# Attention with a causal convolution: whole groups of values, the second query stack in another bank, and the finished output read earlier

## The reference

```python
xn = _rms_norm(x, g_norm) * (1.0 + scale) + shift     # scale, shift = split(cond @ W_emb + b_emb)
q, k, v = heads(xn @ W_qkv)
q = _rms_norm(q, g_q);  k = _rms_norm(k, g_k)
o = softmax(q @ k.T * d ** (-0.5)) @ v                # per head
x = x + (o + o @ W_out)
x = x + causal_depthwise_conv(x, cond) + b            # 4 taps along the rows
```

## Time and profile before

| | before |
|---|---|
| median of 3 runs | 2447.68 us |
| the profiled execution, its own time | 2451.33 us |
| its span, first to last instruction | 2449.4 us |
| PE, share of the span busy | 95% |
| DVE | 84% |
| ACT | 73% |
| POOL | 29% |
| mean granted TensorE clock | 0.989 |

### The profile page before, as it was taken

How to read it: one execution, slowest core, us unless ns; L and a number is a source line. 1 busy time by engine, 2 the same in 40 slices (tenths; PEclk the granted TensorE clock), 3 DMA queues, 4 the chain that set the end, 5 groups by cost and what they waited for, 6 DMA issues and landing times.

```text
span 2449.4 us, 53026 instructions
## 1 busy us (share of the span) xinstructions
PE 2318.2 (95%) x20410; PEld 1499.9 (61%) x20410; DVE 2062.1 (84%) x3212; ACT 1789.7 (73%) x2693; POOL 702.9 (29%) x483
## 2 busy tenths in 40 slices
PE   5799898988899999999999999999999999999889
PEld 0455555555466666666666666666666666666678
DVE  7768988888878888888888888888888888888877
ACT  5467788888777778777777787777777777777732
POOL 1022333332333323333333333333222232322210
PEclk9899999999999999999999999999999999999999
DMA  8999999899999999999999999999998988888971
GB/s 348 312 226 229 193 176 200 182 189 227 204 199 181 204 192 212 181 197 234 200 218 185 213 186 202 195 187 227 192 191 173 182 168 161 176 164 173 193 193 56
DMA packets 1234731, 484.91 MB, mean 198 GB/s; under 512 B 1139632, under 2 KB 1197872, under 8 KB 1232048
## 3 DMA queue, kind: packets, MB, share of 16 engines
q1 hardware_dynamic: 1234480, 481.53, 94.2%
HBM read 137.20 MB, written 56.66 MB: 79 GB/s over the span
## 4 chain that ended last, share of the span: by engine, by line
PE 57%; DVE 19%; issue 8%; ACT 7%; SPq 3%; DMA 2%; POOL 1%; ACTq 0%; POOLq 0%; DVEq 0%
PE proj L1000 33%; PE scores L944 9%; PE values L963 8%; DVE p_pair L1544 7%; DVE neg L1535 7%; PE proj L1033 4%; ACT p_pair L1193 3%; ACT late L1185 2%; DMA w_sb<-w_dram 2%; SPq L746 2%; DVE stage L1566 1%; DVE bias L1538 1%; PE values L976 1%; DVE stage L1570 1%; PE misc L1051 1%
## 5 line engine op out<-in xcount | busy, mean ns | idle before, releaser
L1000 PE MATMUL proj<-w_sb,xn_sb 128*128 128x384 f16 x6144 | 1036.2, 328 | 26.9 <-DMA w_sb<-w_dram 19.6
L1000 PEld LDWEIGHTS proj<-w_sb,xn_sb 128*128 128x128 f16 x6144 | 593.3, 98 | 433.0 <-issue 50.5
L1185 ACT ACTIVATE late<-scores,bias,l_scale 128x1024 f32<-128x1024 f32 x512 | 615.1, 1202 | 311.9 <-DVE bias L1538 292.3
L1544 DVE TENSOR_TENSOR p_pair<-late,p_pair 128x1024 f16<-128x1024 f32 x512 | 616.6, 1246 | 161.3 <-ACT p_pair L1193 160.9
L1535 DVE TENSOR_REDUCE neg<-scores 128x1 f32<-128x1024 f32 x512 | 623.6, 1218 | 113.0 <-PE scores L944 109.8
L1193 ACT ACTIVATE p_pair<-late 128x1024 f16<-128x1024 f32 x512 | 509.8, 1045 | 0.0
L963 PE MATMUL values<-pT,v_pair 128*64 128x256 f16 x6144 | 387.3, 276 | 13.1 <-ACT inv_all L1253 13.1
L944 PE MATMUL scores<-late 64*128 64x512 f16 x3072 | 376.6, 378 | 15.9 <-ACT late L1185 15.5
L963 PEld LDWEIGHTS values<-pT,v_pair 128*64 128x64 f16 x6144 | 317.7, 110 | 93.9 <-issue 74.9
L1435 POOL TENSOR_TENSOR rs<-ms,power 128x16 f32<-128x16 f32 x63 | 183.2, 2908 | 351.8 <-DVE ms L1558 351.5
L1033 PE MATMUL proj<-late,wo 128*128 128x256 f16 x2304 | 267.5, 273 | 3.7 <-issue 3.7
(11 more groups left out here) (179 smaller groups left out, 1925.9 us busy)
## 6 DMA issues: line engine op xcount, KB each, us to landing
w_sb<-w_dram SPq DMA_DIRECT2D x121, 384.0 KB, 4.1
o_dram<-oT_pair SPq DMA_DIRECT2D x124, 128.0 KB, 2.4
out<-late SPq DMA_DIRECT2D x54, 256.0 KB, 2.7
x_in<-in_x SPq DMA_DIRECT2D x25, 512.0 KB, 4.3
late<-in_x SPq DMA_DIRECT2D x25, 512.0 KB, 4.4
wq_raw<-in_L_cond_W_qkv SPq DMA_DIRECT2D x8, 1536.0 KB, 11.5
late<-o_dram SPq DMA_DIRECT2D x12, 1024.0 KB, 6.2
xn_dram<-late SPq DMA_DIRECT2D x21, 512.0 KB, 3.2
```

The lines of the kernel that those rows point to most:

```text
L1000: last = nc.tensor.matmul(proj[:, t % 2, 0:6 * DH], xn_sb[:, t, i * K + c, :], w_sb[:, c, j, :], start=(c == 0 and i == j == 0), stop=(c = ...
L1185: nc.scalar.activation(prob[:, h, :], scores[:, h, :], ACT.Exp, bias=bias[:, s:s + 1], scale=const["l_scale"][:, 0:1], accum_out=total[:, ...
L1544: nc.vector.tensor_tensor(p_pair[:, s % 4, 1, :], prob[:, h, :], p_pair[:, s % 4, 0, :], ALU.subtract).then_inc(lo_done, 1)
```

## The change

It touches the orders of PE, ACT and SP; those of DVE and POOL stay as they are.

- `attend` takes a range of chunks instead of a part. With `outs` a group is done whole (48 matmuls in a row): group 3 of the unit before at pair 2, group 0 at pair 4, group 1 at pair 6, group 2 at the end of pair 7. The halves at the ends of pairs 1, 3 and 5 and the one behind the scores of pair 0 are gone. Units 0 to 7 keep the halves, and the last unit's group 3 too.
- The second stack of half 1 goes into `misc`, behind the whole group 2 at pair 7's end. The projection's wait for it is gone with `fins`, and the stack before it in `misc` no longer waits for `read_out` of half 1.
- `out_transposes` of half 1 moves from pair 6 to pair 4's end, `read_out` of it to the end of ACT's pair 4, `store_out` of it from pair 7 to pair 6 (in front of the loads there).
- `read_inverses` of group 1 moves on ACT from the front of pair 5 to behind its exponents and high parts.

```diff
@@ -864,7 +864,7 @@
                             keep_xn(v)
                         elif xs:
                             store_xn(v)
-                    if p == 6 and fins and last:
+                    if p == 6 and fins:
                         store_out(T - 1, 1 - par, 1)
                     if last and p == 1:
                         load_last_oT(0)
@@ -880,8 +880,6 @@
                         if more and not gives_early(u):
                             load_w(w + 1, 2)
                     if p == 7:
-                        if fins and not last:
-                            store_out(T - 1, 1 - par, 1)
                         if more and not gives_early(u):
                             load_w(w + 1, 3)
                         if not last:
@@ -948,15 +946,15 @@
                             if i == 1 and n == 1:
                                 last.then_inc(qk_done, 1)
 
-            def attend(u, g, par, part):
+            def attend(u, g, par, c0=0, c1=K):
                 n = NG * u + g
-                if part == 0:
+                if c0 == 0:
                     pe.wait_ge(all_ev, n + 1)
                     if g == 0:
                         pe.wait_ge(v_lo, 2 * u + 2)
                     for i in range(4):
                         pe.wait_ge(pT_in[4 * (g % 2) + i], 16 * (2 * u + g // 2 + 1))
-                for c in range(part * KH, (part + 1) * KH):
+                for c in range(c0, c1):
                     for i, j in ((0, 0), (1, 0), (0, 1)):
                         for h in range(2):
                             first = 4 * (g % 2) + h
@@ -965,7 +963,7 @@
                                 v_pair[:, par, 2 * c + h, DH * i:DH * i + DH],
                                 pT[:, first:first + 3:2, j * K + c, :],
                                 start=(c == 0 and i == j == 0), stop=(c == K - 1 and j == 1))
-                if part == 1:
+                if c1 == K:
                     last.then_inc(pv_done, 1)
 
             def inverses(u, g):
@@ -984,7 +982,8 @@
                     if early and t == 1:
                         pe.wait_ge(h_ev, 3 * w - 1)
                     elif t == (2 if early else 0):
-                        need(pe, h_ev, 3 * w)
+                        if fins is None:
+                            need(pe, h_ev, 3 * w)
                     if fins is not None and t < 2:
                         pe.wait_ge(y_ev, 2 * fins + t + 1)
                     if static(w) and w % K == 0:
@@ -1078,6 +1077,7 @@
                 w, T = u + 1, u - K
                 begun = not (static(u) and u == 0)
                 last = u + 1 == U
+                was_whole = u > K
                 for p in range(K):
                     if gives_early(u) and p == 7:
                         project(w + 1, 0, 0, 4)
@@ -1086,9 +1086,11 @@
                         keep_clock(12)
                     score(u, p, par)
                     if p % 2 == 0 and p >= 4:
-                        attend(u, (p - 4) // 2, par, 1)
-                    elif p % 2 == 0 and begun:
-                        attend(u - 1, 2 + p // 2, 1 - par, 1)
+                        attend(u, (p - 4) // 2, par, 0 if outs else KH, K)
+                    elif p == 0 and begun and not was_whole:
+                        attend(u - 1, 2, 1 - par, KH, K)
+                    elif p == 2 and begun:
+                        attend(u - 1, 3, 1 - par, 0 if outs else KH, K)
                     if p % 2 == 1 and p >= 3:
                         inverses(u, (p - 3) // 2)
                     elif p == 1 and begun:
@@ -1098,9 +1100,9 @@
                             project(w + 1, 1, 0, 4)
                         elif not outs:
                             keep_clock(8)
-                        stacks(w, 1, 1, misc[:], (f_ev, 2 * T) if fins else (h_ev, 3 * w + 1))
-                        stacks(w, 1, 0, proj[:, 0, :], (y_ev, 2 * T + 1) if outs else
-                               (qkv_ev, K * w + (9 if gives_early(u) else 7)))
+                        stacks(w, 1, 1, misc[:], (h_ev, 3 * w + 1))
+                        if not outs:
+                            stacks(w, 1, 0, proj[:, 0, :], (qkv_ev, K * w + (9 if gives_early(u) else 7)))
                     if qkv:
                         for t, q0, q1 in (later_quarters if has_early(u) else quarters)[p]:
                             project(w, t, q0, q1, T - 1 if fins else None)
@@ -1115,8 +1117,6 @@
                             out_product(T, par, 0, 1, oT_in, xr, ())
                         else:
                             out_product(T, par, 1, p - 6, oT_in, xr, free1)
-                            if fins and p == 6:
-                                out_transposes(T - 1, 1, (h_ev, 3 * w + 1) if qkv else (f_ev, 2 * T - 1))
                     if last and p < 4:
                         hh = p // 2
                         out_product(T, par, hh, p % 2, oT_in, last_xr[0],
@@ -1127,18 +1127,22 @@
                         if p >= 6:
                             add_x(p - 6, last_xr[1])
                     if qkv and outs and p == 5:
-                        stacks(w, 0, 0, misc[:], (f_ev, 2 * T - 1 if fins else 0))
+                        stacks(w, 0, 0, misc[:], (f_ev, 2 * T if fins else 0))
                         stacks(w, 0, 1, proj[:, 1, :], (qkv_ev, K * w + 8))
                     if fins and p == 1 and not last:
-                        out_transposes(T - 1, 0, (k_ev, u + 1))
-                    if fins and p == 4 and last:
+                        out_transposes(T - 1, 0, (h_ev, 3 * u + 3))
+                    if fins and p == 4:
                         out_transposes(T - 1, 1, (f_ev, 2 * T - 1))
-                    if p % 2 == 1 and p >= 3:
-                        attend(u, (p - 3) // 2, par, 0)
-                    elif p == 1 and begun:
-                        attend(u - 1, 3, 1 - par, 0)
+                    if p % 2 == 1 and p >= 3 and not outs:
+                        attend(u, (p - 3) // 2, par, 0, KH)
+                    elif p == 1 and begun and not outs:
+                        attend(u - 1, 3, 1 - par, 0, KH)
+                    elif p == 7:
+                        attend(u, 2, par)
+                        if qkv:
+                            stacks(w, 1, 0, misc[:], (k_ev, w + 1))
                     if last and p == 1:
-                        out_transposes(T - 1, 0, (k_ev, u + 1))
+                        out_transposes(T - 1, 0, (h_ev, 3 * u + 3))
                     if qkv and not outs and p == 5:
                         stacks(w, 0, 0, misc[:], (qkv_ev, 0))
                         stacks(w, 0, 1, proj[:, 1, :], (qkv_ev, K * w + 8))
@@ -1153,7 +1157,6 @@
             stacks(0, 1, 1, misc[:], (h_ev, 1))
             stacks(0, 1, 0, proj[:, 0, :], (qkv_ev, K - 1))
             in_units(unit, pe)
-            attend(U - 1, 2, 1, 1)
             for hh in range(2):
                 tail_product(0, hh, K - 1)
             tail_product(1, 0)
@@ -1161,9 +1164,9 @@
             tail_transposes(U - K - 1, 0)
             tail_product(1, 1)
             tail_transposes(U - K - 1, 1)
-            attend(U - 1, 3, 1, 0)
+            attend(U - 1, 3, 1, 0, KH)
             tail_transposes(U - K, 0)
-            attend(U - 1, 3, 1, 1)
+            attend(U - 1, 3, 1, KH, K)
             for i in range(2, K):
                 T = U - K + i
                 tail_product(i, 0)
@@ -1298,7 +1301,7 @@
                         read_y(T, 0)
                     if last and p == 4:
                         read_y(T, 1)
-                    if p % 2 == 1 and p >= 3:
+                    if p in (3, 7) or p == 5 and not outs:
                         read_inverses(u, (p - 3) // 2)
                     elif p == 1 and begun:
                         read_inverses(u - 1, 3)
@@ -1315,8 +1318,6 @@
                         if qkv:
                             read_projection(w, 7)
                             squares(w, 1, (h_ss, 2 * w + 1))
-                        if fins and last:
-                            read_out(T - 1, 1)
                     if p == 6:
                         if outs and not last:
                             read_y(T, 0)
@@ -1335,16 +1336,16 @@
                     high(u, p, 1)
                     if 4 <= u < K and p in (1, 3):
                         wo_high(2 * u - 8 + p // 2)
+                    if p == 5 and outs:
+                        read_inverses(u, 1)
                     if qkv and not outs and p == 6:
                         high_halves(w, 1)
                     if p % 2 == 0 and p >= 4:
                         o_high(u, (p - 4) // 2)
                     elif p % 2 == 0 and begun:
                         o_high(u - 1, 2 + p // 2)
-                    if p == 6 and fins and not last:
-                        read_out(T - 1, 1)
                     if qkv and p == 7:
-                        read_stacks(w, 1 - par, 1, 0, 3, proj[:, 0, :])
```

(3 more changed lines are left out.)

## The result

| | before | after |
|---|---|---|
| median of 5 runs | 2448.12 us (2445.06 to 2454.39) | 2428.83 us (2425.20 to 2437.39) |
| the profiled execution, its own time | 2451.33 us | 2425.20 us |
| its span | 2449.4 us | 2423.4 us |
| PE, share busy | 95% | 95% |
| DVE, ACT, POOL | 84%, 73%, 29% | 85%, 74%, 29% |

The ratio is 0.9922, with a 95% interval from 0.9908 to 0.9935: 19 us less (16 to 22.5 by the interval), where 19 was forecast, and clear of the 0.5% too. The two profiled executions lie further apart (26 us) than the medians; of that, 4.9 us are gone before unit 8 starts, where both kernels are the same, so a sum must not be read off the spans alone.

What follows compares the result with a forecast made beforehand. PE was taken as the bound, busy 69.93 of 70.39 us a unit. 22 x 1.01 - 15 x 0.15 + 0.1 - 1.5 = 18.6, rounded 19 us, so the median 2447.68 becomes 2428.7; range 2423 to 2442.

Steps and rivals of the forecast that it cites:

- The price of halves and wholes: On PE, 24 matmuls take 1.43 us and 48 take 2.74; each of three joins saves 0.12 a unit.
- The pairs: PE, pairs 0 to 7: 8.33, 8.06, 11.07, 7.62, 10.54, 8.34, 7.09, 8.33 us; sum 69.38 against 70.39.
- The wait, 0.62: In pair 7, PE's stacks no longer wait for ACT's read of the output: 0.62 us less in a unit.
- What is late next: Whether DVE and ACT, in pairs made shorter or longer, come late for PE; a new wait of 0.15 us at pair 1.
- the lag of 1.0 at pair 6: DVE's first maximum of pair 6 starts 2.54 us behind its scores instead of 1.51.
- its 23.92 us on DVE: DVE's chain from pair 6's first maximum to pair 1's goes on taking 23.92 us.
- the 0.15 at pair 1: PE's output transposes in pair 1 wait for DVE, 0.1 to 0.3 us, taken as 0.15, in units 9 to 23 only.
- The spare at pair 7's scores: Pair 6's second exponent ends at 6.63, pair 7 starts at 7.09: no wait, 0.3 us to spare after a semaphore's latency.
- The rival in which DVE is 0.4 later (8 us): DVE's lag costs 2 us at pair 7's scores and 6 at pair 1's transposes: 2437; chance of the lag 0.18.
- The weights: Pair 0's last quarter lands at 11.6, wanted at 12.7 us after pair 7's scores; no steady wait, 1.5 lost in all.
- the four units: Units 15, 16, 23 and 27, whose last quarter of weights lands late or just in time: 0.4 us more each.
- Edges: Unit 8 takes 0.5 us longer (between 0 and 1.04); the last unit keeps 0.6 of the half taken from pair 0.

Runs made afterwards that it cites:

- group 0 in halves: Changed kernel with group 0 done in halves again (24 matmuls at pair 3's end, 24 behind pair 4's scores): 2426.1 us, one run.
- the earlier output alone: Kernel before, with only the output's second half turned, read and stored earlier: 2447.3 us, ratio 0.9999 (0.9986 to 1.0012).
- inverses in front: Changed kernel with ACT reading group 1's inverses in front of pair 5's exponents again: 2434.1 us, one run.
- whole groups alone: Kernel before, with only the groups done whole as in the change: 2437.6 us, ratio 0.9958 (0.9943 to 0.9973).
- store at pair 7: Changed kernel with the store of the output's second half back in front of the last quarter of weights in pair 7: 2430.2 us, one run.
- quarter behind both stores: Changed kernel with the stores of the output and of group 1 both in front of the last quarter of weights in pair 7: 2433.6 us, one run.

## Why the prediction was right, point by point

*The price of halves and wholes:* 1.43, 2.74, 0.12 a join: right, by the timeline and by group 0 in halves. The comparison of 57 with 60 ns a matmul shows that a longer block is not dearer; as both blocks are of 64 columns, it does not test what such blocks cost beside full-array ones.

*The pairs:* all eight within 0.03 us of the sum, with the wait of pair 1.

*The wait, 0.62:* it went, and with the rest of the change the whole of it came in. What the prediction did not say is that this rests on the other parts: the earlier output alone brings 0.15, and in units 9 to 23 its sum holds only because the read of the inverses moves too (0.40 of the 0.86).

*What is late next:* the lag of 1.0 at pair 6, its 23.92 us on DVE, the 0.15 at pair 1 in units 9 to 23 and none later: right. The spare at pair 7's scores was given as 0.3; the second exponent ended 0.54 ahead of them, 0.4 without the latency. Undoing the read behind exponents costs 0.4 in units 9 to 23, as the same chain says. The rival in which DVE is 0.4 later (8 us) is priced by the same kernel: 6 us at pair 1 as given there, but nearly nothing (pair 6 is 7.11 and not 7.09) instead of 2 us at pair 7, whose spare was larger.

*The weights:* the mis-sized term. I had 1.5 us more of waiting; by the lengths of the units the four took 5.0 us over steady ones before (the slower clock in unit 23 with it), and it went to 2.3 (units 15 and 23 by loads, and 0.2 in unit 18 for DVE), 2.7 less. The step that failed is that the four units would each be later by 0.4. Unit 15 was (by 1.4 in its pair 0, for the burst in front of it), and 16, 23 and 27 were not. How much of this is the change's doing is open: unit 23 is 0.8 to 1.2 us over a steady one in three kernels with the store in pair 6 (changed, inverses in front, group 0 in halves), but 4.5 in the kernel with the output early alone, and 1.7 to 4.5 in four with the store in pair 7 (before, whole groups alone, store at pair 7, quarter behind both stores). The quarter's issue did not come at the forecast 7.9 in units 9 to 13 and 15 either, but at 8.2 to 8.7, since the transposing DMAs in front of it took longer with the store ahead of them; it landed at 12.0 to 12.4 instead of 11.6 and was still in time. In units 16 to 21 it came at 7.4 to 8.2, and in units 23 to 29 at 6.5 to 7.0, 0.7 or more earlier than before.

*Edges:* unit 8 is 0.6 longer (0.5 forecast). The last unit to the end is 0.8 longer where I had 0.6 less. PE's row there and the windows row behind it:

```profile
2264.27 5.28 PE L1032 MATMUL proj<-late,wo 128*128 128x256 f16 x24 [3.60 <-POOL late L1473]
```

```profile
2264.30:2270.00 5.70, 5.70 (x28) 0.51 0.96 215
```

and the windows row of the kernel before at the same place:

```profile
2292.70:2296.00 3.30, 3.30 (x30) 1.00 1.12 225
```

It waits 3.60 for POOL's work on the late load, where it waited 3.73 before (that row names no releaser), but this time the clock fell behind it, and 24 matmuls that take 2.78 took 5.28. I had not counted that; in the kernel before, a wait of nearly the same length left the clock alone. Without these 2.5 us the end would be some 1.7 shorter.

*Sum of the profiled pair:* 22.5 in units 9 to 30, less 0.6 and 0.8 at the edges, and 4.9 from the unchanged units in front. The first three make 21, the forecast was 19: steady units 19.9 (forecast 20.0), the weights 2.7 gained (forecast 1.5 lost), the edges 1.4 lost (forecast 0.1 gained). So the steady units were foreseen, and two terms were missed in opposite ways; that the medians too are 19 apart is in part luck, since their interval reaches from 16 to 22.5.

## What to carry to other kernels

Where one engine is full and the others run a chain beside it, work out the chain's start behind that engine's in each step, not the busy shares: here it gave each of eight intervals to 0.03 us, and told that a wait is worth 0.15 alone and 0.6 with room made in the same step. Parts of a change that share such a chain do not add up, so a test of each alone must be joined by one of all but one. Before moving a transfer to an emptier place in the queue's order, look at what is issued right behind it there; the time of the transfer moves into the next ones. And compare repeated units, not whole times, when single edits are to be told apart.

## What the runs showed of the hardware that I had not expected

- POOL's power on 128x16 took 3.81 us where DVE's low parts already ran when it started, and 2.90 where they began 0.8 us (changed kernel) or 1.25 us (before) after it, or where DVE's reductions ran beside it. The cause is open.
- The clock of TensorE fell behind a wait of 3.60 us in the changed kernel's last unit (0.51 of full speed over 5.7 us), not behind one of 3.73 in the same place of the kernel before, and behind 10 of 22 waits of about 2.9 us. Each fall cost 1.7 us or more.
- Two transposing DMAs held SP for 6.4 us with three transfers (of 256 to 512 KB) in front of them and for 8.2 with four. Over units 9 to 14 of the ten kernels that load one quarter in pair 6 it is 5.4 to 6.0 us with two in front, 5.3 to 7.1 with three and 6.9 to 9.1 with four.
